# Differential attention and channel mixing on one core: moving the prologue's products, the maxima's steps and the last group's stages

## The chip, the cores and the metric

The kernel runs on 1 core of one Trainium2 chip. The metric is device microseconds of one execution; the median of the runs is compared. All times below are microseconds unless marked ns.

## The reference, cut to what matters

```python
# x: (2, 1024, 128); 16 heads, each with two score maps of width d = 4 and values of width 8
q, k, v = x @ Wq * d ** -0.5, x @ Wk, x @ Wv            # split into 32 score heads, 16 value heads
probs = softmax(where(causal, q @ k.T, -inf))            # 32 maps per batch, 1024 x 1024
attn = (probs[:, :, 0] - lam * probs[:, :, 1]) @ v       # lam from lq1, lk1, lq2, lk2
attn = attn * rsqrt(mean(attn ** 2) + eps) * rms_w * (1 - LAMBDA_INIT)
x = layernorm(x + attn @ Wo)
x_prev = shift x by one token                             # zeros ahead of token 0
r = sigmoid((mu_r * x + (1 - mu_r) * x_prev) @ W_r.T)
k = relu((mu_k * x + (1 - mu_k) * x_prev) @ W_k.T) ** 2
out = layernorm(x + r * (k @ W_v.T))
```

## The kernel before, in words

Each engine's program is written out by hand, in order; engines meet at counting semaphores only. The 64 score maps are worked off in 32 **pairs** (n = 0 to 31; two pairs are one group g, numbers pr 0 and 1; groups 0, 1, 14 and 15 are written out, the others stand in a loop of two groups, so four pairs for one turn of it).

**Splitting.** The scores must be exact, so q and k are cut in three bf16 parts (`high` and `middle` on ACT, `remainder` and `low` on DVE) and written to DRAM (`q_rows`, `k_rows`) as rows that SP loads again per pair (`load_max_rows` into `qm`, `km`, L288; `load_exp_rows` into `qe`, `ke`, L294). SP writes the q parts of the first 32 partitions, ACT the k parts (`write_parts`, L308), and SP then the rest of batch 0 and batch 1.

**Maxima.** For each pair there are NU = 9 units (`MAX_UNITS`): PE computes coarse scores into one of two PSUM buffers `mx` (`max_unit`, L557; unit m waits until unit m - 2 is reduced) and DVE reduces them (`max_unit`, L1047, one TENSOR_REDUCE over 1024 columns for each unit). Units 0 and 1 also add a mask. Then DVE runs `combine` (the maxima of all nine), `split_high` and `split_low` (row maximum in two bf16 parts); PE turns them (`turn_maxima`, L603), ACT copies them to `max_rows` (L877) and SP places them in `qe` by two small transfers (`place_maxima`, L300).

**Bursts.** A pair has NQ = 9 bursts b. PE does in each: a unit of maxima (unit 8 of pair n + 1 at b = 0, units 0 to 7 of pair n + 2 at b = 1 to 8, EARLY = 8), two score tiles in `ex` (L609; three PSUM banks in a ring, `ex_slot`), and a sum burst (L628) for the exponentials of four bursts ago (LAG = 4). ACT takes the exponential of each tile (L960), POOL masks the diagonal ones. Between these come, at fixed bursts: `take_sums` at b = 3 (ACT copies the sums of pair n - 1), `turn_maxima` for pair n + 1 at MAXIMA_AT = 4 behind the scores and its ACT copy behind both exponentials of that burst, `turn_sums` and `store_sums` at TURN_AT = 6, `invert` at INVERT_AT = 1 of the second pair of a group (DVE). A slot of the ring is kept for the turned maxima and two for the turned sums.

**SP's queue.** For each pair SP issues in this order, and waits in order: `load_max_rows(n + 2)`, `load_exp_rows(n + 1)` (once pair n - 1 is scored), `place_maxima(n + 1)` (once ACT has copied them). So the loads for pair n + 2 stand behind the placing for pair n.

**DVE's order** at the maxima of a pair: unit 8, `combine`, unit 0 of the next but one, `split_high`, unit 1, `split_low`, then units 2 to 7:

```python
                if m == NU - 1:
                    combine(n + 1, 1 - pr)
                if m == NU:
                    split_high(n + 1)
                if m == NU + 1:
                    split_low(n + 1)
```

**Prologue.** x is turned on PE; q and k are projected and split, chunk by chunk (ACT and DVE copy one chunk of xT of each batch); the 16 products for the values (L682) and three turned weights (L689) come next, and only then the maxima of pair 0 and 1 (17 units). `wait` on v_copied stands ahead of the first `turn_maxima`.

**Last group and tail.** In group 15 the stages of batch 0 are put beside the bursts by the tables `beside`: `turn_attn`, `project`, `turn_x1`, `ffn_k`, `ffn_r`, `ffn_o` on PE, `norm_attn`, `apply1`, `square_k`, `norm_ffn`, `apply2` on DVE, the roots on POOL. The token shift is done by two accumulated products, with weights scaled by mu and by 1 - mu (`w_cur`, `w_prev`). Pair 31's sums come in two halves (`normalise_half`, `root_half`, `place_half`). Then batch 1 (chunks 2 and 3) follows as a chain: turn, project, norm, turn, k, r, o, norm, store. `turn_attn(2)` stands between the last sum bursts.

Of the kernel before, what the change touches and what calls it, by code (L numbers as in the profile page):

```python
# [12 lines left out]
P = 128  # L13
# [77 lines left out]
TAKE_AT, TURN_AT, MAXIMA_AT, INVERT_AT = 3, 6, 4, 1  # L91
# [3 lines left out]
EX_BANKS = 3  # L95

# [21 lines left out]
def build(nc, x, Wq, Wk, Wv, Wo, lq1, lk1, lq2, lk2, rms_w, W_r, W_k, W_v, mu_r, mu_k, out):  # L118
# [24 lines left out]
    with ExitStack() as ctx:  # L143
# [12 lines left out]
        w_cur = sb("w_cur", [P, 2, P])  # L156
        w_prev = sb("w_prev", [P, 2, P])
# [82 lines left out]
        def mx_of(n, pr, m):  # L240
# [11 lines left out]
                   x1_turned x1_copied k_scored r_scored k_relued r_gated k_squared o_scored z_scaled z_ready  # L252
                   stats2 rooted1 rooted2 half_set half_steps half_rooted shifted1 shifted2 quad_seen
                   den_inverted values_seen norm_seen norm_steps lam_paired out_ready
# [53 lines left out]
        def write_parts(eng, which, b, own, done):  # L308

            subs = slice((b * P + own.start) // D, (b * P + own.stop) // D)  # L310
            for part, need in ((0, "hi_done"), (1, "mid_done"), (2, "lo_done")):
                eng.wait_ge(s[need], 4 * (b + 1))
                for w in which:
                    for i in (i for i, term in enumerate(TERMS) if term[w] == part):
                        eng.dma_start((q_parts, k_parts)[w][subs, :, i, :], parts[w][part][own, b, :])\  # L315
                            .then_inc(done, 16)

        @block.sync
        def _(sp):
# [23 lines left out]
            write_parts(sp, (0,), 0, slice(0, HEAD), s["rows_head"])  # L343
# [4 lines left out]
            write_parts(sp, (0, 1), 0, slice(HEAD, P), s["rows_b0"])  # L348
            fill_rows(1, s["rows_b1"])
            write_parts(sp, (0, 1), 1, slice(0, P), s["rows_b1"])  # L350
# [34 lines left out]
        def _(pool):  # L385
# [156 lines left out]
            beside = {(0, 2): [(root1, 0)], (0, 8): [(root1, 1)], (1, 7): [(root2, 0)], (1, 8): [(root_half, 0)]}  # L542
# [8 lines left out]
            for stage, arg in ((root2, 1), (root_half, 1), (root1, 2), (root1, 3), (root2, 2), (root2, 3)):  # L551
                stage(arg)
# [3 lines left out]
        def _(pe):  # L556
# [46 lines left out]
            def turn_maxima(n, bank):  # L603

                pe.wait_ge(s["max_split"], n + 1)
# [56 lines left out]

            pe.wait_ge(s["ident"], 5)
            for b in range(B):
                pe.wait_ge(s[f"x_in{b}"], 16)
                for t in range(b * NB, (b + 1) * NB):
                    last = pe.transpose(wide[t // 4][:, P * (t % 4):P * (t % 4 + 1)], x_tok[:, t, :], identf[:])
                    if t % 4 == 3:
                        last.then_inc(s["xt_done"], 1)
                if b == 0:  # L670
                    pe.wait_ge(s["wqk_in"], 32)
                for ch in (2 * b, 2 * b + 1):
                    pe.wait_ge(s["xt_copied_a" if ch % 2 == 0 else "xt_copied_d"], b + 1)
                    for w, weights in enumerate((wq_sb, wk_sb)):
                        m = 2 * ch + w
                        wait(pe, s["rest_done"], m - 3)
                        pe.matmul(narrow[m % 4], weights[:], xT[:, BANK * ch:BANK * (ch + 1)], start=True,  # L677
                                  stop=True).then_inc(s["proj_done"], 1)
            pe.wait_ge(s["wv_in"], 16)
            pe.wait_ge(s["rest_done"], 2 * NCH)  # L680
            for t in range(NT):
                last = pe.matmul(narrow[t // 4][:, P * (t % 4):P * (t % 4 + 1)], xT[:, P * t:P * (t + 1)],  # L682
                                 wv_sb[:], start=True, stop=True)
                if t % 4 == 3:
                    last.then_inc(s["v_done"], 1)
# [11 lines left out]
            for m in range(NU):  # L697
                max_unit(0, 0, m)
# [573 lines left out]
```

## Time and profile before

| | |
|---|---|
| median of 3 runs | 464.49 (463.41 to 464.81) |
| profiled execution, its own time | 463.41 |
| its span in the profile | 461.6, so 1.8 lie around it |
| mean granted TensorE clock | 0.941 |
| first exponential, last reduction of a unit | 53.7, 388.6 |
| busy: PE, DVE, ACT, POOL | 397.3, 393.2, 352.2, 223.4 |

A row of the timeline gives start, duration, engine, line and tiles, and in brackets the idle time of the engine before it and who ended it. Merged rows (x7) hold several instructions in turn. A landing time counts from the issue of a transfer to its last byte. The ends of matmuls are modelled.

### The profile page before, as it was taken

The numbers are of one execution on the slowest core, as the hardware profiler recorded it, in microseconds if no ns is written. First come the engines' busy times: TensorE is split into PE (matmuls) and PEld (weight loads), VectorE is DVE, ScalarE is ACT, GpSimd is POOL, SyncE is SP. The second block draws the span as 40 slices with busy tenths as digits, with TensorE's granted clock in tenths as the row PEclk, the third lists the DMA queues.
The fourth block names the chain that finished last, engine by engine and source line by source line (L and its number), as shares of the span: only waits on it lengthen the run. The fifth ranks groups of instructions, "written<-read, shape, count | busy, mean of one in ns | idle before, by whom it ended". The sixth has DMA issues, their size and how long they took to land.

```text
span 461.6 us, 16566 instructions
## 1 busy us (share of the span) xinstructions
PE 397.3 (86%) x5717; PEld 192.1 (42%) x5717; DVE 393.2 (85%) x554; ACT 352.2 (76%) x735; POOL 223.4 (48%) x514
## 2 busy tenths in 40 slices
PE   5475699999989999999999999999999999995682
PEld 2152234444444444444444444444444444553452
DVE  1459999999999999999999999999999998435443
ACT  2360389899989989999989999998999999763233
POOL 7200122356555656555555556565656565663312
PEclk9795589999999999999999999999999999999578
DMA  5468311111111111111111211111111110000101
GB/s 134 171 217 323 134 49 48 49 48 50 48 49 48 46 46 46 46 47 47 46 48 55 51 49 50 46 56 49 55 47 46 48 48 26 3 1 2 45 1 45
DMA packets 21390, 28.44 MB, mean 62 GB/s; under 512 B 4960, under 2 KB 9952, under 8 KB 21232
## 3 DMA queue, kind: packets, MB, share of 16 engines
q1 hardware_dynamic: 20688, 27.45, 19.8%
q10 hardware_dynamic: 672, 0.59, 0.4%
q8 instruction: 19, 0.31, 0.3%
q14 instruction: 11, 0.09, 0.1%
HBM read 20.39 MB, written 9.47 MB: 65 GB/s over the span
## 4 chain that ended last, share of the span: by engine, by line
PE 70%; ACT 11%; DVE 9%; issue 5%; ACTq 2%; DMA 1%; POOL 0%; POOLq 0%; DVEq 0%
PE acc L652 32%; PE mx L570 14%; ACT e_buf L960 9%; PE ex L622 9%; DVE part_max L1054 5%; PE ex L660 3%; PE mx L579 2%; PE ex L677 2%; PE ex L606 2%; PE mx L742 1%; DMA x_tok<-in_L_attn_x 1%; PE mx L743 1%; PE mx L727 1%; ACTq L315 1%; PE mx L762 1%
## 5 line engine op out<-in xcount | busy, mean ns | idle before, releaser
L1054 DVE TENSOR_REDUCE part_max<-mx 128x2 f32<-128x1024 f32 (+2 forms) x288 | 336.7, 1214 | 5.9 <-PE mx L570 3.8
L960 ACT ACTIVATE e_buf<-ex 128x512 f32<-128x512 f32 x576 | 304.8, 599 | 43.7 <-PE ex L622 41.0
L491 POOL TENSOR_SCALAR_AFFINE_SELECT e_buf<-e_buf 128x256 f32<-128x256 f32 x256 | 99.5, 407 | 175.2 <-ACT e_buf L960 175.2
L652 PE MATMUL acc<-e_buf,v_grp 128*32 128x256 f32 x2756 | 181.0, 351 | 0.1
L622 PE MATMUL ex<-qe,ke 26*128 26x512 bf16 (+3 forms) x768 | 139.3, 332 | 0.6 <-ACT e_buf L960 0.6
L570 PE MATMUL mx<-km,qm 29*128 29x128 bf16 (+3 forms) x1280 | 117.4, 270 | 15.6 <-DVE part_max L1054 13.0
L570 PEld LDWEIGHTS mx<-km,qm 26*128 26x128 bf16 (+1 forms) x1280 | 41.8, 93 | 118.3 <-DVE part_max L1054 79.3
L652 PEld LDWEIGHTS acc<-e_buf,v_grp 128*32 128x32 f32 x2756 | 64.6, 108 | 52.6 <-issue 36.3
L622 PEld LDWEIGHTS ex<-qe,ke 26*128 26x128 bf16 x768 | 45.0, 91 | 12.2 <-ACT e_buf L960 3.0
L474 POOL TENSOR_TENSOR r_rms<-sq_eps,minus_half 128x16 f32<-128x16 f32 x15 | 43.6, 2906 | 0.1
L579 PE MATMUL mx<-mask,pick 32*128 32x128 bf16 x512 | 25.9, 220 | 0.0
L881 ACT COPY max_rows<-ex 32x128 bf16<-32x128 bf16 x32 | 7.9, 248 | 13.8 <-PE ex L606 13.8
L579 PEld LDWEIGHTS mx<-mask,pick 32*128 32x128 bf16 x512 | 17.9, 96 | 0.0
L606 PE MATMUL ex<-identb,turn_max 128*128 128x128 bf16 x32 | 7.4, 231 | 12.1 <-ACT e_buf L960 11.3
L520 POOL TENSOR_TENSOR rs<-ve,minus_half 128x4 f32<-128x4 f32 x8 | 8.2, 1024 | 18.8 <-DVE ve L1145 18.8
L660 PE MATMUL ex<-identf,o_rows 128*128 128x128 f32 x62 | 13.6, 300 | 3.0
L888 ACT COPY o_rows<-acc 128x256 f32<-128x256 f32 x31 | 11.5, 372 | 4.5 <-PE acc L652 2.5
L479 POOL TENSOR_TENSOR attn_n<-attn,r_rms 128x32 f32 (+1 forms) x60 | 12.9, 247 | 3.7 <-POOL r_rms L474 3.7
L436 POOL COPY v_grp<-v_all 128x128 f32 (+1 forms) x16 | 4.6, 290 | 18.6 <-ACT v_all L864 18.6
L677 PE MATMUL ex<-xT,wq_sb 128*128 128x512 f32 x8 | 6.4, 894 | 6.8 <-ACT xT L836 6.8
L606 PEld LDWEIGHTS ex<-identb,turn_max 128*128 128x128 bf16 x32 | 3.1, 96 | 21.7 <-issue 17.0
L660 PEld LDWEIGHTS ex<-identf,o_rows 128*128 128x128 f32 x62 | 6.2, 140 | 12.1 <-ACT e_buf L960 11.9
(134 smaller groups left out, 269.9 us busy)
## 6 DMA issues: line engine op xcount, KB each, us to landing
qm<-q_rows SPq DMA_DIRECT2D x32, 128.0 KB, 2.6
km<-k_rows SPq DMA_DIRECT2D x32, 128.0 KB, 2.7
qe<-q_rows SPq DMA_DIRECT2D x32, 128.0 KB, 2.5
ke<-k_rows SPq DMA_DIRECT2D x32, 128.0 KB, 2.7
q_rows<-part_q SPq DMA_DIRECT2D x6, 256.0 KB, 5.5
k_rows<-part_k SPq DMA_DIRECT2D x6, 256.0 KB, 5.4
q_rows<-part_q SPq DMA_DIRECT2D x6, 192.0 KB
k_rows<-part_k SPq DMA_DIRECT2D x6, 192.0 KB
```

The lines of the kernel that those rows point to most:

```text
L474: pool.tensor_tensor(r_rms[:], sq_eps[:], minus_half[:], ALU.pow).then_inc(s["norm_steps"], 1)
L479: pool.tensor_tensor(attn_out(n, c, ab), attn_chunks[:, c, ab], r_rms_chunks[:, c, ab], ALU.mult).then_inc(s["attn_ready"], 1)
L491: pool.affine_select(out=e, in_=e, compare_op=ALU.is_ge, fill=0.0, base=0, pattern=[[0, PAIR], [1, P]], channel_multiplier=-1)\
L570: last = pe.matmul(bank[:, jj, col:col + P * nk], qm[pr][rows, P * qb:P * (qb + 1)], km[pr][rows, P * kb:P * (kb + nk)], start=i == 0, sto ...
L579: last = pe.matmul(bank[:, jj, :].rearrange("p (a t) -> p a t", a=4)[:, :, own], pick[rows, c, :], cols, start=False, stop=c == 3, skip_gr ...
L606: pe.transpose(ex[:, bank, :].bitcast(BF16)[:, 0:P], turn_max[:].rearrange("p e r -> p (e r)"), identb[:]).then_inc(s["max_turned"], 1)
L622: scored = pe.matmul(ex[:, ex_slot(b, i) % EX_BANKS, col:col + w], ke[pr][rows, P * kb:P * (kb + 1)], qe[pr][rows, q1 - w:q1], start=col = ...
L652: last = pe.matmul(out, v, e, start=first, stop=over, skip_group_check=True)
L660: last = pe.transpose(turned[:, P * i:P * (i + 1)], o_rows[pr][:, P * i:P * (i + 1)], identf[:])
L677: pe.matmul(narrow[m % 4], weights[:], xT[:, BANK * ch:BANK * (ch + 1)], start=True, stop=True).then_inc(s["proj_done"], 1)
L960: nc.scalar.activation(e_buf[:, b, i, :], ex[:, ex_slot(b, i) % EX_BANKS, :], ACT.Exp).then_inc(s["exped"], 1)
L1054: nc.vector.tensor_reduce(target, mx_of(n, pr, m)[:].rearrange("p s (a b) -> p s a b", a=a), AX.X, ALU.max).then_inc(s["maxed"], 1)
```

## The change

- Prologue: SP and ACT share the first writes in another way (8 and 4 instead of 6 and 6); DVE, not ACT, copies chunk 2 of xT; the maxima's units begin directly behind the projections. The value products stand one by one behind units 3 to 16 on PE, in the order of chunks 2, 3, 0, 1; the weights are turned behind unit 13, now in `acc`; `turn_maxima(0)` comes behind unit 12. ACT copies also unscaled weights (`w_both`). On DVE the last five splitting steps and lambda's steps stand between and behind the units.
- Steady part: `combine`, `split_high` and `split_low` one unit later; MAXIMA_AT 4 to 5, TURN_AT 6 to 7, INVERT_AT 1 to 2.
- Last group: for batch 0 DVE mixes the tokens (`mix_x`), so k and r need one product each; stages are placed anew.
- Tail: the last sums ahead of `turn_attn(2)`; `turn_x1(3)` ahead of `ffn_o(2)`; both halves normalised before chunk 2's norm; the last `apply2` shared by ACT and DVE (two tiles each).

```diff
-TAKE_AT, TURN_AT, MAXIMA_AT, INVERT_AT = 3, 6, 4, 1
+TAKE_AT, TURN_AT, MAXIMA_AT, INVERT_AT = 3, 7, 5, 2
+V_ORDER = (2, 3, 0, 1)
...
-            write_parts(sp, (0,), 0, slice(0, HEAD), s["rows_head"])
+            for w, part in ((0, 0), (1, 0), (0, 1)):
+                write_part(sp, w, part, 0, slice(0, HEAD), s["rows_head"])
...
+                if c == NCH - 1:
+                    sp.wait_ge(s["rest_ready"], 1)
...
-            beside = {(0, 2): [(root1, 0)], (0, 8): [(root1, 1)], (1, 7): [(root2, 0)], (1, 8): [(root_half, 0)]}
+            beside = {(0, 2): [(root1, 0)], (0, 7): [(root1, 1)], (1, 7): [(root2, 0)], (1, 8): [(root_half, 0)]}
...
-            for stage, arg in ((root2, 1), (root_half, 1), (root1, 2), (root1, 3), (root2, 2), (root2, 3)):
+            for stage, arg in ((root_half, 1), (root2, 1), (root1, 2), (root1, 3), (root2, 2), (root2, 3)):
...
+            def turn_weights():
+                pe.wait_ge(s["w_in"], 16 * 4)
+                pe.wait_ge(s["v_copied"], 2)
+                for i in range(3):
+                    last = pe.transpose(acc[:, P * i:P * (i + 1)], wf_sb[:, i, :], identf[:])
+                last.then_inc(s["wt_done"], 1)
...
+            values = {3 + i: [(V_ORDER[i // 4], i % 4)] for i in range(12)}
+            values[NU + EARLY - 2] = [(V_ORDER[3], 0), (V_ORDER[3], 1)]
+            values[NU + EARLY - 1] = [(V_ORDER[3], 2), (V_ORDER[3], 3)]
+            for u in range(NU + EARLY):
+                max_unit(0, u // NU, u % NU)
+                for ch, i in values.get(u, []):
+                    project_v(ch, i)
+                if u == NU + 3:
+                    turn_maxima(0, 2)
+                if u == NU + 4:
+                    turn_weights()
+            pe.wait_ge(s["wt_scaled"], 1)
             pe.wait_ge(s["v_copied"], NCH)
...
+                if ch < 2:
+                    pe.wait_ge(s["x_mixed"], 2 * ch + 1)
+                    pe.matmul(main[ch], w_both[:, 1, :], x_mixed[ch][:, 1, :], start=True, stop=True)\
+                        .then_inc(s["k_scored"], 1)
+                    return
...
+                    if ch < 2:
+                        last = pe.matmul(o, x_mixed[ch][:, 0, P * i:P * (i + 1)], w_both[:, 0, :], start=True, stop=True)
+                        continue
...
-                      (0, 4): [(project, 1)], (0, 8): [(turn_x1, 0)], (1, 0): [(ffn_k, 0)], (1, 1): [(turn_x1, 1)],
+                      (0, 4): [(project, 1)], (0, 8): [(turn_x1, 0)], (1, 0): [(turn_x1, 1)], (1, 1): [(ffn_k, 0)],
...
-            turn_attn(2)
             sum_burst(NG - 1, 1, 1, NQ - 2)
             sum_burst(NG - 1, 1, 1, NQ - 1)
             turn_sums(NPAIR + 1, 0, last_acc)
+            turn_attn(2)
             project(2)
             turn_attn(3)
             project(3)
...
+            turn_x1(2)
+            ffn_k(2)
+            ffn_r(2)
+            turn_x1(3)
+            ffn_o(2)
+            ffn_k(3)
+            ffn_r(3)
+            ffn_o(3)
...
+                last = nc.scalar.copy(w_both[:, i, :], src)
...
-            copy_attn(2)
             take_half(1)
             store_half(1)
+            copy_attn(2)
             copy_attn(3)
             apply1(2)
             copy_x1(2)
+            apply1(3)
             relu_k(2)
-            apply1(3)
             gate_r(2)
...
-            apply2(3)
+            apply2(3, 2)
...
+            late = {0: [(remainder, 6), (low, 5)], 1: [(remainder, 7), (low, 6)], 2: [(low, 7)],
+                    NU: [(combine, 0, 0)], NU + 1: [(split_high, 0)], NU + 2: [(split_low, 0)]}
+            for u in range(NU + EARLY):
+                max_unit(0, u // NU, u % NU)
+                for step, *args in late.get(u, []):
+                    step(*args)
+                if u == 4:
+                    lambda_dots()
+            lambda_pairs()
...
-                if m == NU - 1:
+                if m == NU:
                     combine(n + 1, 1 - pr)
-                if m == NU:
+                if m == NU + 1:
                     split_high(n + 1)
-                if m == NU + 1:
+                if m == NU + 2:
                     split_low(n + 1)
...
+            def mix_x(ch):
+                b, t0 = ch * BANK // S, ch * BANK % S
+                dve.wait_ge(s["xcol_set"], 1)
+                dve.wait_ge(s["x1_copied"], ch + 1)
+                wait(dve, s["x_mixed"], 2 * ch)
+                now, past = x1T[:, b, 1 + t0:1 + t0 + BANK], x1T[:, b, t0:t0 + BANK]
+                nc.vector.tensor_tensor(x_step[:], now, past, ALU.subtract).then_inc(s["x_stepped"], 1)
+                dve.wait_ge(s["x_stepped"], ch + 1)
+                for i in (1, 0):
+                    nc.vector.scalar_tensor_tensor(out=x_mixed[ch][:, i, :], in0=x_step[:], scalar=mu[:, i:i + 1],
+                                                   in1=past, op0=ALU.mult, op1=ALU.add).then_inc(s["x_mixed"], 1)
...
             apply1(1)
+            mix_x(0)
             invert(NG - 2, 0)
+            mix_x(1)
             square_k(0)
             norm_ffn(0)
             square_k(1)
+            norm_ffn(1)
             normalise_half(0)
-            norm_ffn(1)
+            apply2(0)
+            normalise_half(1)
             place_half(0)
-            apply2(0)
-
-            normalise_half(1)
+            place_half(1)
             norm_attn(2)
-            place_half(1)
             apply2(1)
```

## Rows read from the trace of the kernel before

**Rows 1.** Part 1 of the page: busy time of each engine, share of the span.
```profile
PE 397.3 (86%) x5717; PEld 192.1 (42%) x5717; DVE 393.2 (85%) x554; ACT 352.2 (76%) x735; POOL 223.4 (48%) x514
```

**Rows 2.** Timeline, DVE, one pair: start, us, engine, line, operation, tiles, [idle before].
```profile
226.47 8.06 DVE L1054 TENSOR_REDUCE part_max<-mx 128x2 f32<-128x1024 f32 x7
...
234.57 0.22 DVE L1060 TENSOR_REDUCE row_max<-part_max 128x16 f32<-128x64 f32 x1
...
234.80 1.23 DVE L1054 TENSOR_REDUCE part_max<-mx 128x8 f32<-128x1024 f32 x1
```

**Rows 3.** Timeline, PE: unit 0 at burst 1 of pair 1 and of pair 29.
```profile
66.34 0.40 PE L570 MATMUL mx<-km,qm 29*128 29x128 bf16 x8
...
377.91 0.34 PE L570 MATMUL mx<-km,qm 29*128 29x128 bf16 x6
```

**Rows 4.** Timeline, SP queue, two pairs; last, landing times of km's loads there.
```profile
217.22 1.19 SPq L305 DMA_DIRECT2D qe<-max_rows  x2
...
219.32 0.54 SPq L292 DMA_DIRECT2D km<-k_rows  x1
...
228.26 1.19 SPq L305 DMA_DIRECT2D qe<-max_rows  x2
...
230.67 0.54 SPq L292 DMA_DIRECT2D km<-k_rows  x1
...
DMA to landing us min/median/max: 2.6/2.6/2.6
```

**Rows 5.** Timeline, ACT, around burst 4 of the same pair.
```profile
226.49 1.58 ACT L960 ACTIVATE e_buf<-ex 128x512 f32<-128x512 f32 x3
...
227.94 0.25 ACT L881 COPY max_rows<-ex 32x128 bf16<-32x128 bf16 x1
```

**Rows 6.** Timeline, pair whose km lands late, with that load's landing time.
```profile
129.84 0.54 SPq L292 DMA_DIRECT2D km<-k_rows  x1
...
133.98 0.40 PE L570 MATMUL mx<-km,qm 29*128 29x128 bf16 x8 [0.73 <-DVE part_max L1054]
...
134.74 1.23 DVE L1054 TENSOR_REDUCE part_max<-mx 128x8 f32<-128x1024 f32 x1 [0.52 <-PE mx L579]
...
139.60 1.19 SPq L305 DMA_DIRECT2D qe<-max_rows  x2
...
DMA to landing us min/median/max: 4.0/4.0/4.0
```

**Rows 7.** Timeline, start of the kernel, with the landing time of rms_col.
```profile
21.69 0.60 SPq L292 DMA_DIRECT2D km<-k_rows  x1
...
34.17 10.28 DVE L1054 TENSOR_REDUCE part_max<-mx 128x8 f32<-128x1024 f32 x9 [0.99 <-PE mx L579]
...
45.34 0.61 SPq L352 DMA_DIRECT2D rms_col<-w_bounce  x1
...
54.06 0.61 PE L570 MATMUL mx<-km,qm 29*128 29x128 bf16 x8 [0.38 <-DVE part_max L1054]
...
DMA to landing us min/median/max: 5.0/5.0/5.0
```

**Rows 8.** Chain that ended last, in the last group: start, us, what.
```profile
403.49 0.86 PE mx L743 x2
...
414.80 0.22 PE mx L754 x2
...
439.03 0.87 PE mx L734 x4
```

**Rows 9.** Timeline, last group and tail.
```profile
414.25 0.69 DVE L1183 TENSOR_TENSOR xT<-part_k,x 128x512 f32<-128x512 f32 x1
...
421.78 0.25 DVE L1199 RECIPROCAL r_den<-o_tok 128x16 f32<-128x16 f32 x1 [4.72 <-ACT o_tok L910]
...
426.78 0.76 PE L719 MATMUL mx<-identf,attn_n 128*128 128x128 f32 x4 [4.39 <-DVE attn_n L1223]
...
457.36 1.65 ACT L936 ACTIVATE v_all<-xT,shift,rs 128x128 f32<-128x128 f32 x4 [3.17 <-POOL shift L527]
```

More of the change, by code:

```diff
@@ L156, in build @@
         w_cur = sb("w_cur", [P, 2, P])
+        w_both = sb("w_both", [P, 2, P])
+        x_step = sb("x_step", [P, BANK])
+        x_mixed = [sb(f"x_mixed{i}", [P, 2, BANK]) for i in range(2)]
         w_prev = sb("w_prev", [P, 2, P])
@@ L603, in turn_maxima @@
             def turn_maxima(n, bank):
+                if isinstance(n, int) and n == 0:
+                    pe.wait_ge(s["v_copied"], 1)
                 pe.wait_ge(s["max_split"], n + 1)
@@ L661, in turn_sums @@
                 last.then_inc(s["acc_turned"], 1)
-            pe.wait_ge(s["ident"], 5)
[L664 to L685, printed above, removed]
-            pe.wait_ge(s["w_in"], 16 * 4)
-            pe.wait_ge(s["v_copied"], 1)
-            for i in range(3):
-                last = pe.transpose(narrow[0][:, P * i:P * (i + 1)], wf_sb[:, i, :], identf[:])
@@ L690, in _, with turn_x, project_qk @@
-            last.then_inc(s["wt_done"], 1)
+            def turn_x(ch):
+                for t in range(4 * ch, 4 * ch + 4):
+                    last = pe.transpose(wide[ch][:, P * (t % 4):P * (t % 4 + 1)], x_tok[:, t, :], identf[:])
+                last.then_inc(s["xt_done"], 1)
+            def project_qk(m):
+                ch = m // 2
+                wait(pe, s["rest_done"], m - 3)
+                pe.matmul(narrow[m % 4], (wq_sb, wk_sb)[m % 2][:], xT[:, BANK * ch:BANK * (ch + 1)], start=True,
+                          stop=True).then_inc(s["proj_done"], 1)
@@ L820, in _ @@
             project(3)
-            for ch in (2, 3):
-                turn_x1(ch)
-                ffn_k(ch)
-                ffn_r(ch)
-                ffn_o(ch)
+            turn_x1(2)
[6 more added lines that the diff above has]
+            ffn_o(3)
         @block.scalar
@@ L1047, in max_unit @@
+            for i in range(2):
+                nc.vector.memset(part_max[i][:], NEG).then_inc(s["parts_set"], 1)
+            nc.vector.memset(turn_max[:, 2:], 0.0).then_inc(s["parts_set"], 1)
+            copy_x(1)
+            remainder(0)
+            for m in range(1, 4):
+                remainder(m)
+                low(m - 1)
+            low(3)
+            copy_x(2)
+            copy_x(3)
             def max_unit(g, pr, m):
@@ L1130, in _ @@
             group(NG - 2, 0)
-            for b in range(3):
+            for b in range(NU - EARLY + 3):
                 burst(NG - 1, 1, 0, b)
```

186 lines of the change are left out of this document (98 added, 88 removed).

## The prediction, made before the changed kernel was run

> **What bounds the kernel now.** I read the page first, then DVE's timeline over the steady part, then the queue of SP beside PE and ACT, and last the chain of waits for the tail. On the page no engine stands out: PE is busy for 86% of the span, DVE for 85% [rows 1]. The timeline shows where each is the bound. From unit 2 of one pair to the next pair's maxima DVE has no gap: seven reductions take 8.06, so one starts every 1.14, and `combine` begins at 234.57, when the last has ended, the next unit 0.23 later [rows 2]. That is a steady part in which DVE is full. From unit 0 at burst 1 of pair 1 to that of pair 29 PE needs 377.91 - 66.34 = 311.57 for 28 pairs, 11.13 each [rows 3]. These are 312 of 461.6. Before them lies the prologue (66), behind them the last pairs and the tail (84).
>
> One more loop runs through every pair, and the reader is to see it because no engine's busy share shows it: ACT copies the turned maxima, SP places them, and only then does SP issue qm and km for the pair after next; PE needs these at its burst 1. Placing starts at 217.22 and the km load is issued 2.10 later, at 219.32; where the program's loop turns (once in four pairs) it is 2.41 [rows 4]. The load lands 2.6 after its issue [rows 4].
>
> How close this loop is, one pair tells: there km took 4.0 to land. It was issued at 129.84, PE could start unit 0 at 133.98 only, 0.14 after the landing, and DVE then stood idle for 0.52 [rows 6]. So a normal km comes 4.0 - 2.6 = 1.4 earlier and has some 0.9 to spare before DVE stands still.
>
> **The steady part, where the change costs.** Three things move by a burst. `combine` goes behind unit 0 of the next pair: it need no longer wait for unit 8 to end. Now 8.06 / 7 = 1.15 per unit, plus 0.04, plus 0.23 stand for it; behind another unit I put 0.15 for it, so DVE would save 0.1 to 0.2 in each pair, if DVE stayed the bound. The Trainium skill, VectorE: DVE Perf Modes, section The DRAIN you can't avoid, says that the next operation waits for the pipe to empty with or without a semaphore; by that rule nothing would be saved here. The rows speak for a little, and it will not matter if the loop below binds. `invert` keeps its price.
>
> The turn of the maxima goes from burst 4 to burst 5. Its ACT copy then stands behind two more exponentials. Three of them in a row take 1.58 and one lasts 0.60, so one starts every 0.49, and the copy at 227.94 starts behind the third, bound by ACT, not by the turn [rows 5]. Two more are 0.98. They are no added work, but they stand ahead of the copy, and behind the copy stand, on SP, the two placing transfers and then qm and km of the pair after next.
>
> So the loop is, counted from PE's start of unit 0 at burst 1:
> - to the placing now: 139.60 - 133.98 = 5.62 [rows 6]; this is PE's own bursts 1 to 3 and `take_sums`, then ACT, so it does not depend on DVE;
> - two exponentials more: 0.98 [rows 5];
> - placing to the issue of km: 2.10, with the loop's turn 0.31 more in one pair of four, 0.08 on average [rows 4];
> - landing 2.6 [rows 4] and PE's start 0.14 after it [rows 6].
>
> Sum 11.52 per pair. Today the same sum is 10.54, below the 11.13 of the pair, so the loop has slack of 0.6; after the change it is above and becomes the bound: 11.52 - 11.13 = 0.39 more per pair. The loads for pairs 3 to 31 are gated so; from burst 1 of pair 1 to that of pair 29 are 28 pairs: **+10.9**. Bounds for the pair: 11.35 (landing 2.5, the copy a little nearer) and 11.7 (a late landing as in rows 6 now and then), so +6 to +16. `turn_sums` at burst 7 and its place in the ring of `ex` have the same structure as now, a burst later, and cost nothing: the copies on ACT lie one in each of the bursts 3, 5 and 7; cover gone, they would be 0.3 each. POOL gets the inverted sums a burst later and masks nothing at bursts 3 to 6, which is enough.
>
> **The prologue, where it gains.** Rows of pair 0 are loaded from 21.69 and 2.7 more on they are there, near 24.4, but the first reduction is at 34.17 and the nine take 10.28 [rows 7]. After the change units can start near 25. DVE does five splitting steps of 0.69 between the first three units (3.4) and lambda's steps (0.8), so its 17 units end at about 25 + 17 x 1.14 + 4.4 = 49, not 53.9. That is 4.8 earlier, but two things come later than that. SP's queue is a row of issues without a gap up to rms_col, 45.34 + 0.61 = 45.95 [rows 7]; the sharing of the first writes (8 issues on SP, 4 on ACT) makes the last of them 0.2 earlier, and so all behind it. Placing for pair 0 can start at 45.7; km for pair 2 is issued 2.1 later and lands at 50.5 or, as much of batch 1 is still being written (rms_col took 5.0 to land [rows 7]), near 51. DVE also waits for rms_col, to about 50.1. The copies of the values (the last two products stand behind units 15 and 16), the weights and the two extra copies to `w_both` end near 48 and are hidden by that. So PE's burst 1 of pair 0 moves from 54.06 [rows 7] to about 50.8. Bounds: 48.5 if the rows land at once, 52 if they wait for all writes. At burst 1 of pair 1 this leaves **-3.3** (-5 to -2).
>
> **Last group and tail, where it gains more.** In each chunk of batch 0 the second k product (0.86) and four of eight r products (0.22 each) fall away [rows 8]: 2 x (0.86 + 0.88) = 3.5 on PE, which is the chain there. DVE gets three operations of 128x512 for each chunk; a like one takes 0.69 [rows 9], 2.1 in all, and it is idle for several us between its steps there; they come between the copy of x1 and ffn_k, and one burst more has been put there. `turn_x1(1)`, one burst sooner, comes up to 0.5 before its x1. That leaves -3.0 at the first half's sums. Then the last sums run at once: now `turn_attn(2)` waits for 4.39 [rows 9] with the last two sum bursts behind it. But the second half's store, some 8 earlier, is not what ends last: DVE has `norm_ffn(1)`, both halves and `apply2(0)` in a row. From normalising half 0 to `turn_attn(2)` are 426.78 - 421.78 = 5.0 today [rows 9], with `norm_ffn(1)` in between. After the change half 1 (I put 1.8 for its seven small steps) and `apply2(0)` (1.1, as ACT's four tiles take 1.65 [rows 9]) come before it too: 7.9 from the start of that norm near 417.2 (3.0 before where it could start now), so `turn_attn(2)` at 425.1, only 1.7 earlier. What follows is shorter: projecting 2 no longer waits behind half 1, and `turn_x1(2)`, now at 439.03 behind `project(3)` [rows 8], starts about 434.4: -4.6. `turn_x1(3)` ahead of `ffn_o(2)` hides its copy (0.6 with the hand-over): -5.2. The last four tiles on ACT take 1.65 [rows 9]; with two on DVE -0.8. Sum **-5.9** (-7.5 to -4). PE stands idle for over 3 ahead of `turn_attn(2)` after the change as before it, so I take the tail's products at the same granted clock. Pair 30 itself is free of the loop: -0.1.
>
> **Sum.** -3.3 + 10.9 - 0.1 - 5.9 = +1.6. The profiled execution took 463.41 (span 461.6 and 1.8 around it), so it would be 465.0; the median shown, 464.49, lies 1.1 above it, so **466.1** there. A change of about 0.3% (1.4) is what a measurement of this kernel can tell from none.
>
> **Rivals.**
> - A, DVE stays the bound (0.12). If the placing is sooner than I say, a pair takes 10.95 by DVE's saving: 28 x -0.18 = -5.0, with -9.3 at the ends -14.3: 450.2. For it: DVE has no gap now [rows 2]. Against it: rows 6, where 1.4 of lateness already stops it. The Trainium skill, Perfetto Trace Analysis, section Identifying the Most-Contended Engine, would have one take work off the busiest engine first; by it this case would come out. [...]
> - B, the loop just fits (0.18). Its slack today is 0.6 by my sum and 0.9 by rows 6; were it 0.98, pairs would stay at 11.13, and only the ends count: 464.5 - 9.3 = 455.2.
> - C, slower (0.12): the placed maxima come late too. Half of `place_maxima` is issued 0.6 behind its start; it must land by burst 0, some 1.15 before burst 1, which by the loop is 4.84 behind the placing. If it takes over 3.7 from the start of the placing, each 0.1 beyond it costs 2.8 in all. With a pair at 11.8: +18.8 - 9.3 = +9.5: 474.0.
> - The change does not do what it says (0.03): the units start no earlier, as SP's rows are late: 3 more than forecast, 469.
>
> **Chances.** Forecast 0.55, with a range of its own of 462.5 to 469.5: within it 0.30 slower, 0.18 same, 0.07 faster. With A and B faster, C and the last case slower: faster 0.37, same 0.18, slower 0.45. The range for all is 454.5 to 470: it takes in B and most of the forecast's cases and leaves A and most of C out.
>
> **What would show it.** Unit 0 at burst 1: 28 periods of about 11.5, DVE idle about 0.4 to 0.6 in each pair just before it, with PE named, and PE idle there with km's landing 0.1 earlier; SP's placing 6.6 after PE's burst 1. First exponential near 50. Last group: k with one product, turn_attn(2) behind all sums, one shared last apply. Periods of 11.13 or less, with no idle time at burst 1, make the forecast wrong by 10 or more; a span unchanged with such short periods would put the fault in my ends.

## The result, and where the time went

The changed kernel takes **472.44** us (470.75 to 474.43), the kernel before 464.09 beside it on the same chip: a ratio of 1.018, 95% interval 1.014 to 1.022. I had forecast slower by 1.6, that is 466.1, with a range up to 470.0: the side was right, the time lies 2.4 above the range. The profiled execution has a span of 470.6 (before: 461.6). Burst 1 of pairs 1 and 29 cuts both into three parts:

| part | before | after | difference | forecast |
|---|---|---|---|---|
| start to burst 1 of pair 1 | 66.34 | 65.20 | -1.1 | -3.3 |
| 28 pairs | 311.57 (11.13 each) | 327.17 (11.68 each) | +15.6 | +10.9 |
| burst 1 of pair 29 to the end | 83.69 | 78.23 | -5.5 | -6.0 |

The page of the changed kernel, parts 1 and 5 (busy time; costliest groups with their idle time before):

```profile
PE 411.2 (87%) x5697; PEld 193.0 (41%) x5697; DVE 400.3 (85%) x563; ACT 351.6 (75%) x734; POOL 224.7 (48%) x514
...
L1112 DVE TENSOR_REDUCE part_max<-mx 128x2 f32<-128x1024 f32 (+2 forms) x288 | 340.5, 1214 | 27.1 <-PE mx L590 20.0
...
L581 PE MATMUL mx<-km,qm 29*128 29x128 bf16 (+3 forms) x1280 | 118.2, 272 | 19.9 <-DMA km<-k_rows 10.6
```

Beside [rows 1] hardly a busy share has moved. What is new is the last field: DVE, which had no gap in the pair of [rows 2], stands idle for 27 us before its reductions (5.9 in the kernel before), mostly because PE is late, and PE is late because of km. Part 4, the chain that ended last, says the same; at 14% the landing of km is its largest piece (in the kernel before, DMA had 1% of the chain and PE 70%):

```profile
PE 36%; issue 15%; DMA 15%; DVE 12%; SPq 10%; ACT 10%; POOL 1%; ACTq 1%; DVEq 1%; POOLq 0%
```

One turn of the loop, from the timelines of PE, SP's queue and DVE (start, us, engine, line, what, idle time before):

```profile
218.37 0.40 PE L581 MATMUL mx<-km,qm 29*128 29x128 bf16 x8 [0.30 <-DMA km<-k_rows]
...
225.05 1.19 SPq L310 DMA_DIRECT2D qe<-max_rows  x2
...
227.15 0.54 SPq L297 DMA_DIRECT2D km<-k_rows  x1
...
229.88 0.40 PE L581 MATMUL mx<-km,qm 29*128 29x128 bf16 x8 [0.29 <-DMA km<-k_rows]
...
230.63 1.23 DVE L1112 TENSOR_REDUCE part_max<-mx 128x8 f32<-128x1024 f32 x1 [0.47 <-PE mx L590]
```

In the same pair on ACT:

```profile
222.32 2.56 ACT L1011 ACTIVATE e_buf<-ex 128x512 f32<-128x512 f32 x5
224.72 0.26 ACT L884 COPY max_rows<-ex 32x128 bf16<-32x128 bf16 x1
```

From PE's burst 1 to the placing 6.68 (it was 5.62, [rows 6]), to the issue of km 2.10, to the next burst 1 2.73: 11.51. DVE then has its 0.47 of idle time, with PE named. The combine does overlap now: the next unit starts 0.13 behind it, where [rows 2] have 0.23 (DVE, same pair):

```profile
220.26 0.21 DVE L1118 TENSOR_REDUCE row_max<-part_max 128x16 f32<-128x64 f32 x1
220.39 1.22 DVE L1112 TENSOR_REDUCE part_max<-mx 128x8 f32<-128x1024 f32 x1
```

So both the wait and the overlap that the forecast named are there; the sizes are taken up below.

The head, PE between the last maxima units of the prologue and at the first bursts of pair 0, then ACT's last copy of values:

```profile
47.56 0.61 PE L581 MATMUL mx<-km,qm 26*128 26x256 bf16 x4
48.10 1.22 PE L692 MATMUL ex<-wv_sb,xT 128*128 128x128 f32 x4
49.26 0.61 PE L581 MATMUL mx<-km,qm 26*128 26x256 bf16 x4
49.79 1.22 PE L692 MATMUL ex<-wv_sb,xT 128*128 128x128 f32 x4
51.74 0.50 PE L581 MATMUL mx<-km,qm 26*128 26x128 bf16 x6 [0.72 <-issue]
...
52.01 0.76 PE L581 MATMUL mx<-km,qm 26*128 26x128 bf16 x10
52.55 0.33 PE L590 MATMUL mx<-mask,pick 32*128 32x128 bf16 x2
...
53.67 0.60 PE L581 MATMUL mx<-km,qm 29*128 29x128 bf16 x8
```

A merged row carries the shape of its first instruction. The sixteen products in the rows at 51.74 and 52.01 are the eight of unit 8 (burst 0) and the eight of unit 0 (burst 1), whose mask follows at 52.55; the first of unit 0 starts at 52.12. The row at 53.67 is unit 1, at burst 2. So burst 1 of pair 0 comes at 52.12, where the kernel before has 54.06 [rows 7] and the forecast 50.8.

```profile
51.05 0.58 ACT L904 COPY v_all<-ex 128x512 f32<-128x512 f32 x1 [2.54 <-PE ex L692]
```

The same products in the kernel before, ahead of the maxima, and in the changed one (groups by line, busy us and mean ns of one; each product is two records):

```profile
L682 PE MATMUL ex<-wv_sb,xT 128*128 128x128 f32 x24 | 2.9, 278 | 2.0 <-DVE rest L1014 2.0
L682 PE MATMUL acc<-wv_sb,xT 128*128 128x128 f32 x8 | 1.1, 275 | 0.0
```

```profile
L692 PE MATMUL ex<-wv_sb,xT 128*128 128x128 f32 x24 | 8.8, 487 | 0.1
L692 PE MATMUL acc<-wv_sb,xT 128*128 128x128 f32 x8 | 3.2, 502 | 0.0
```

And the changed kernel's window from 44 to 48 (busy time of PE, PEld, DVE, ACT, POOL; then the granted clock):

```profile
44.00:48.00 4.00, 4.00 (x18) 1.96 (x17) 3.17 (x3) 1.85 (x9) 0.00 (x0) 0.50 1.05 403
```

PE is full there, at the lower of its two levels (1.2 GHz), and DVE waits for it: its 17 units end at 51.1 and not at 49. The last two products end at 51.0, the copy stands behind them until 51.6, and PE waits for the copy before the first burst of pair 0. What that wait costs is taken up below.

### The profile page after: what moved, and what is told of

The parts are those of the page before. It is cut to its first block, busy times and chain, and to the rows that moved or that the text cites. A ratio compares the mean times of both kernels' runs of the same rounds, so it can differ in the third digit from the quotient of the medians.

```text
span 470.6 us, 16533 instructions
## 1 busy us (share of the span) xinstructions
PE 411.2 (87%) x5697; PEld 193.0 (41%) x5697; DVE 400.3 (85%) x563; ACT 351.6 (75%) x734; POOL 224.7 (48%) x514
## 4 chain that ended last, share of the span: by engine, by line
PE 36%; issue 15%; DMA 15%; DVE 12%; SPq 10%; ACT 10%; POOL 1%; ACTq 1%; DVEq 1%; POOLq 0%
DMA km<-k_rows 14%; PE acc L665 10%; PE mx L581 9%; ACT e_buf L1011 7%; DVE part_max L1112 7%; SPq L310 5%; PE ex L635 4%; SPq L296 3%; PE mx L590 2%; PE ex L692 1%; SPq L318 1%; DMA x_tok<-in_L_attn_x 1%; DVE turn_max L1125 1%; ACT max_rows L884 1%; PE mx L805 1%
## 5 line engine op out<-in xcount | busy, mean ns | idle before, releaser
L1112 DVE TENSOR_REDUCE part_max<-mx 128x2 f32<-128x1024 f32 (+2 forms) x288 | 340.5, 1214 | 27.1 <-PE mx L590 20.0
L502 POOL TENSOR_SCALAR_AFFINE_SELECT e_buf<-e_buf 128x256 f32<-128x256 f32 x256 | 100.8, 412 | 166.7 <-ACT e_buf L1011 166.7
L635 PE MATMUL ex<-qe,ke 26*128 26x512 bf16 (+3 forms) x768 | 147.7, 335 | 0.7 <-ACT e_buf L1011 0.5
L635 PEld LDWEIGHTS ex<-qe,ke 26*128 26x128 bf16 x768 | 46.2, 91 | 22.4 <-ACT e_buf L1011 9.0
L490 POOL TENSOR_TENSOR attn_n<-attn,r_rms 128x32 f32 (+1 forms) x60 | 12.8, 245 | 3.7 <-POOL r_rms L485 3.7
L1249 DVE SCALAR_TENSOR_TENSOR part_k<-part_k,mx 128x512 f32<-128x512 f32 x4 | 2.8, 688 | 8.6 <-PE mx L805 8.6
L463 POOL TENSOR_TENSOR o_scaled<-o_tok,r_lam 128x256 f32<-128x256 f32 x15 | 9.5, 632 | 1.2
```

The source lines that it names most:

```text
L490: pool.tensor_tensor(attn_out(n, c, ab), attn_chunks[:, c, ab], r_rms_chunks[:, c, ab], ALU.mult).then_inc(s["attn_ready"], 1)
L502: pool.affine_select(out=e, in_=e, compare_op=ALU.is_ge, fill=0.0, base=0, pattern=[[0, PAIR], [1, P]], channel_multiplier=-1)\
L635: scored = pe.matmul(ex[:, ex_slot(b, i) % EX_BANKS, col:col + w], ke[pr][rows, P * kb:P * (kb + 1)], qe[pr][rows, q1 - w:q1], start=col = ...
L1112: nc.vector.tensor_reduce(target, mx_of(n, pr, m)[:].rearrange("p s (a b) -> p s a b", a=a), AX.X, ALU.max).then_inc(s["maxed"], 1)
```

## Experiments

The executions of a table row ran beside executions of the kernel before (medians 463.7 to 464.0); "burst 1" is that of pair 1, the period is over 28 pairs, "rest" is from burst 1 of pair 29 to the end, all from the profiled execution alone. How far such a single reading scatters, the table itself shows: with the same prologue and the same order on SP burst 1 comes at 65.20 (the changed kernel), 65.67, 63.03 and 64.81, and with the same tail the rest takes 77.6 to 79.4.

| kernel | median | ratio, 95% | burst 1 | period | rest |
|---|---|---|---|---|---|
| steady_old | 457.80 | 0.981 to 0.988 | 65.67 | 11.18 | 77.9 |
| steady_new | 480.42 | 1.027 to 1.037 | 66.51 | 11.70 | 84.6 |
| loads_first | 455.91 | 0.979 to 0.985 | 63.59 | 11.13 | 78.9 |
| before_loads_first | 463.53 | 0.997 to 1.002 | 65.29 | 11.10 | 84.1 |
| turn_old | 468.78 | 1.007 to 1.015 | 63.03 | 11.64 | 78.8 |
| max4_late | 478.27 | 1.020 to 1.037 | 64.81 | 11.88 | 79.4 |
| lf_max4 | 476.73 | 1.022 to 1.032 | 64.36 | 11.89 | 78.7 |
| lf_combine_old | 458.01 | 0.977 to 0.993 | 64.34 | 11.17 | 79.0 |
| lf_values_short | 454.82 | 0.970 to 0.987 | 63.26 | 11.13 | 77.6 |
| lf_values_early | 455.54 | 0.980 to 0.988 | 63.29 | 11.13 | 78.5 |
| lf_two_products | 460.03 | 0.988 to 0.994 | 64.39 | 11.13 | 82.5 |
| lf_tail_order_old | 458.37 | 0.984 to 0.993 | 64.61 | 11.13 | 80.9 |
| best_a | 454.39 | 0.976 to 0.981 | 64.79 | 11.10 | 77.9 |
| best_b | 455.16 | 0.976 to 0.982 | 63.92 | 11.11 | 78.9 |

### Is it the steady part?

**steady_old** is the changed kernel with

```diff
-TAKE_AT, TURN_AT, MAXIMA_AT, INVERT_AT = 3, 7, 5, 2
+TAKE_AT, TURN_AT, MAXIMA_AT, INVERT_AT = 3, 6, 4, 1
-                if m == NU:        combine; NU + 1: split_high; NU + 2: split_low
+                if m == NU - 1:    combine; NU: split_high; NU + 1: split_low
```

> The changed kernel with the five schedule positions of its steady loop put back (turn, maxima, invert at 6, 4, 1 in place of 7, 5, 2; the combine, split high and split low behind the last scoring unit of a half group as before); prologue and tail stay changed. Theory (the steady loop costs the time): the period of a pair falls from 11.69 to 11.13 us, 28 pairs give back 15.6 us, span near 455 and time near 457, about 7 us faster than the kernel before (ratio 0.985). Rival (the later positions are innocent, the cost comes in with the prologue's or the clock's state and stays with the chip through the loop): the period stays at 11.6 to 11.7 and the time near 472.

**steady_new** is the kernel before with the same edit the other way round.

> The kernel before with only the five schedule positions of the steady loop changed. Theory: the period of a pair goes from 11.13 to 11.69 us, +15.6 us over 28 pairs, time near 480 (ratio 1.033). Rival (the loss needs the new prologue or tail beside it): under 470.

Measured: 457.80 and 480.42, periods 11.18 and 11.70. The steady part costs some 15 whichever prologue and tail stand beside it. (11.18 and not 11.13 holds two pairs of 12.5 and 12.4 right behind the prologue: PE waited 1.24 for a late km at 78.16, and then had a granted clock of 0.58 from 79 to 83. In the other 26 pairs the period is 11.09.)

### Is it the loop through SP?

**loads_first** changes only the order of SP's issues in the changed kernel, for pair 0 too:

```diff
+            load_max_rows(sp, 2, 0)
             place_maxima(sp, 0, 0, 0)
...
-                    load_max_rows(sp, n + 2, pr)
                     load_exp_rows(sp, n + 1, 1 - pr)
+                    load_max_rows(sp, n + 3, 1 - pr)
                     place_maxima(sp, n + 1, 1 - pr, g + pr)
```

> The changed kernel with one edit on the SP queue: the loads of the query and key rows of pair n+3 are issued ahead of the placing of the maxima of pair n+1, right behind the loads of its exponential rows, in place of behind it. The loop that my forecast names (first burst of a pair, placing of the maxima, issue of the next key rows, landing, first burst of the next pair) is then cut, since the key rows no longer wait for the placing. Loop theory: the period falls from 11.69 to 11.1 us or less (the bound is VectorE again), so 15 us or more off, time near 456. Rival (the later positions cost through VectorE's or the ring's order or through TensorE, and the late key rows are only a symptom): the period stays above 11.5 and the time above 467.

**before_loads_first** is the same edit of the kernel before.

> The same edit of the SP queue in the kernel before. Theory (in the kernel before VectorE bounds the loop and the key rows land in time): within 1 us of the kernel before, 463 to 465. Rival (its key rows were also late in some pairs, so that the order of the queue costs there too): 2 to 5 us faster, period under 11.05.

Measured: 455.91 (-16.5 on the changed kernel) and 463.53 (no change). The placing is as late as before, 6.60 to 6.72 behind burst 1, but km is issued ahead of it and PE starts without it. DVE is without a gap again:

```profile
224.43 8.16 DVE L1116 TENSOR_REDUCE part_max<-mx 128x2 f32<-128x1024 f32 x7
232.51 0.21 DVE L1122 TENSOR_REDUCE row_max<-part_max 128x16 f32<-128x64 f32 x1
232.63 1.22 DVE L1116 TENSOR_REDUCE part_max<-mx 128x8 f32<-128x1024 f32 x1
233.77 0.38 DVE L1129 CAST turn_max<-row_max 128x16 bf16<-128x16 f32 x1
```

So the loss of the steady part is the loop, all but some 0.03 a pair: with it cut in both, the period is 11.13 here and 11.10 in the kernel before. That the same edit gives nothing before shows that its loop had slack.

### Which of the moves closes the loop?

**turn_old** is the changed kernel with 3, 6, 5, 1: only the maxima's turn and the combine stay late.

> The changed kernel with the sums' turn and the inversion back at 6 and 1, and only the turn of the maxima (5) and the combine's place as in the change. Loop theory: the placing of the maxima still stands two exponentials later, so the period of a pair stays at 11.6 to 11.7 us. Rival (the delay of the sums' turn, with its place in the ring of score banks, has a part in it): period under 11.5.

Period 11.64, so the turn of the maxima closes the loop. The 11.64 holds two long pairs, 12.54 and 12.75, around a late km; over pairs 7 to 28, which have none in either kernel, it is 11.55 against 11.62 in the changed kernel. So the sums' turn and the inversion have a small part, some 0.06 a pair. It shows in every second pair: there SP places 6.73 behind burst 1 in the changed kernel and 6.55 in turn_old. In those pairs of the changed kernel PE waits at burst 4 for POOL, which gets the inverted sums a burst later, in 11 pairs from 5 to 27:

```profile
234.00 0.64 PE L665 MATMUL acc<-e_buf,v_grp 128*32 128x256 f32 x8 [0.24 <-POOL v_grp L447]
```

In turn_old that wait is 0.04 at most.

**max4_late** is the changed kernel with 3, 7, 4, 2: the maxima's turn early, the combine late.

> The changed kernel with only the turn of the maxima back at burst 4; combine and splits stay a unit later. Loop theory: the placing comes 5.6 to 6.1 us behind PE's burst 1 in place of 6.7, the sum of the loop is 10.6 to 11.1, so the period falls to 11.1 to 11.2 (some 14 us off, time near 458). Rival (TensorE now waits at burst 4 for the low split, which VectorE does a unit later, and the pair pays that on TensorE): period 11.3 or more.

Measured 478.27, period 11.88: the rival, and worse than it said. The placing is back at 5.64 to 5.76, so the loop is short again, yet PE now waits for the low split (PE's timeline):

```profile
235.03 0.23 PE L619 MATMUL ex<-identb,turn_max 128*128 128x128 bf16 x1 [1.24 <-DVE turn_max L1130]
```

and behind that wait the clock goes (windows; PE, PEld, DVE, ACT, POOL, clock):

```profile
233.00:235.00 2.00, 0.80 (x16) 0.29 (x6) 2.00 (x6) 1.89 (x5) 1.85 (x5) 1.00 0.00 0
235.00:237.00 2.00, 1.97 (x23) 0.79 (x25) 1.48 (x2) 0.88 (x3) 1.62 (x5) 0.63 0.01 2
237.00:239.00 2.00, 2.00 (x30) 0.85 (x22) 1.67 (x2) 1.52 (x4) 0.22 (x1) 0.51 0.10 26
239.00:241.00 2.00, 2.00 (x27) 0.78 (x24) 1.89 (x3) 1.57 (x4) 0.22 (x1) 1.00 0.35 108
```

From pair 5 on, pairs of 11.26 alternate with pairs of 12.8. In ten of the odd ones the granted clock falls to the lower level, 1.2 GHz, for some 3 us behind a wait of 1.10 to 1.24. In two of them, pairs 9 and 23, it stayed at 1.00 behind waits of 1.23 and 1.24, and these took 11.58: so the clock costs 1.2 in a pair in which it falls. After the waits of up to 0.92 in the other pairs it never fell. **lf_max4** asks whether the loop has a part in that, by taking it away (loads first, and 3, 7, 4, 2):

> The kernel with the loads first and the turn of the maxima back at burst 4, combine and splits a unit later. Theory (TensorE's wait for the low split, and the granted clock behind it, cost the pair): TensorE still waits about 1 us at burst 4 and the pair takes 11.5 to 11.9. Rival (with burst 4 the loop was still the cause): 11.1 to 11.2.

Period 11.89, and in eleven odd pairs the clock falls as before (0.72 from 211 to 217); in the one left, pair 15, it stays up behind a wait of 1.21, and that pair takes 11.58. The loop has no part in it. A late combine needs a late turn of the maxima, or PE stops and is slowed.

### What is the combine's move worth?

**lf_combine_old** is loads_first with combine and splits at their old places:

> The kernel with the loads first on the SP queue (pair 11.12 us, VectorE without idle time), with only the combine and the two splits back at their old places. My forecast put 0.1 to 0.2 us per pair of VectorE's time on the move, if VectorE stays the bound: then the pair takes 11.22 to 11.32 here. Rival (the move only shifts the same cost: 0.11 less at the combine, 0.17 more at the following cast): 11.05 to 11.12.

Period 11.17, between the two: 0.04 per pair, about 1 us in all, in place of 0.1 to 0.2. The overlap of the combine saves 0.1 (0.13 for 0.22 from its start to the next unit's). Part of that is lost again at the splits: the low split takes 0.21 in place of 0.16. The cast of `split_high`, which the expectation's rival names, is not where it goes: it takes 0.35 with the combine back at its old place and 0.37 in loads_first. It takes 0.21 in the kernel before and in best_a below, which has all the old positions, so its length comes with the later turns; why is open. The placing 0.08 later in every second pair of this run (6.79 for 6.72) was not followed up.

### Why the head gave 1.1 and not 3.3

**lf_values_short** is loads_first with quarter-length value products:

```diff
-                xT[:, P * t:P * (t + 1)], wv_sb[:],
+                xT[...].bitcast(BF16)[upper halves], wv_sb[:].bitcast(BF16)[upper halves],
```

> The kernel with the loads first, in which each value product is made from the upper halves of its operands as bf16, a product of a quarter of the passes: this makes the values inexact, and takes some 4.5 of the 6.3 us that the sixteen products take between the first maxima at the half clock. If the products there are why burst 1 of pair 0 came at 52 to 53.7 us and not at 50.8 as I forecast, it comes at 50 to 51 now. Rival (rows and queue of SP, or the maxima placed, set it): 52 or later.

The "52 to 53.7 us" of this expectation, and the 52.3 of the next one, are a misreading of mine: they are the starts of unit 1 at burst 2. Burst 1 of pair 0 comes at 50.79 in loads_first and at 52.12 in the changed kernel. The row of twelve in loads_first holds the last four products of unit 8 and the eight of unit 0:

```profile
50.58 0.86 PE L585 MATMUL mx<-km,qm 26*128 26x128 bf16 x12
```

With the short products it comes at 50.61, next to nothing sooner:

```profile
50.02 0.61 PE L639 MATMUL ex<-qe,ke 26*128 26x512 bf16 x2 [2.29 <-DMA qe<-max_rows]
50.61 0.61 PE L585 MATMUL mx<-km,qm 29*128 29x128 bf16 x8
```

PE and DVE are done sooner (DVE's last unit of the prologue starts at 46.46 and not at 48.58), but PE then waits 2.29 for the placed maxima. So the rival named the cause, if not its number: the placed maxima hold the scores of burst 0 at 50.02, where products and copy had them at 50.55. (The full products take 12.0 of PE in the changed kernel and not the 6.3 of my expectation.)

**lf_values_early** is loads_first with the values in the order 0, 1, 2, 3, the first eight products ahead of the first unit and the others behind units 3 to 10.

> The kernel with the loads first, with the value products of chunks 0 and 1 ahead of the first maxima, while TensorE waits for the first rows at 20 to 23.5 us, and those of chunks 2 and 3 behind units 3 to 10, none behind the last two units. The last value copy then no longer stands between the maxima and the first scores of pair 0. If TensorE's products and that copy set burst 1 of pair 0, it comes 1 to 2 us earlier than in the kernel with the loads first (52.3) and the time is 454 to 455. Rival (the placed maxima's landing sets it at once): within 0.5 us, time 455.9.

The same picture with exact values: burst 1 of pair 0 at 50.79, as in loads_first, of pair 1 at 63.29, time 455.54, within 0.5 of loads_first: the rival. PE again waits for the placed maxima:

```profile
50.66 0.61 PE L639 MATMUL ex<-qe,ke 26*128 26x512 bf16 x2 [1.87 <-DMA qe<-max_rows]
```

Behind that the clock is at its lower level:

```profile
48.00:52.00 4.00, 1.83 (x31) 1.36 (x34) 3.10 (x9) 0.72 (x2) 0.00 (x0) 0.50 0.63 192
52.00:56.00 4.00, 3.85 (x35) 1.53 (x39) 4.00 (x7) 3.89 (x9) 1.94 (x5) 0.50 0.15 49
56.00:60.00 4.00, 4.00 (x51) 1.52 (x43) 2.92 (x3) 2.62 (x7) 0.00 (x0) 0.60 0.00 1
60.00:64.00 4.00, 3.81 (x70) 1.57 (x70) 3.93 (x5) 3.35 (x7) 1.04 (x3) 1.00 0.16 45
```

PE is full from 52 to 60, at half its clock until about 59. In the changed kernel the lower level lasts until 62.1, 10.0 behind burst 1 of pair 0, and pair 0 takes 13.08; in the kernel before it lasts until 62.0, 7.9 behind it, and pair 0 takes 12.28. That fits the 0.8 of the head's gain that is gone between pairs 0 and 1: what starts earlier runs longer at the slow clock. It is read from the windows; no run holds the clock apart.

### The two terms of the tail

**lf_two_products** takes the branches for batch 0 out of `ffn_k` and `ffn_r`:

```diff
-                if ch < 2:
-                    pe.matmul(main[ch], w_both[:, 1, :], x_mixed[ch][:, 1, :], start=True, stop=True)
```

> The kernel with the loads first, with the k and r products of batch 0 made twice as before (with the current and with the previous token) and the mixing on VectorE kept but not waited for. My forecast put 3.0 us of the tail's gain on the single products: from burst 1 of pair 29 to the end 78.2 becomes 81. Rival (TensorE is not the chain there): under 79.

**lf_tail_order_old** puts the four engines' last steps back in their old order:

> The kernel with the loads first, with the order of the last steps put back on TensorE, ScalarE, VectorE and GpSimd (attention chunk 2 turned ahead of the last two sum bursts, the halves normalised around the norm of chunk 1, each chunk of the last two finished before the next begins); single products and the shared last apply stay. My forecast put 2.2 us on this order: 78.2 becomes 80.4. Rival (the order only moves idle time): under 79.

Measured 82.5 and 80.9 against 78.9: the single products are worth 3.6, the order 2.0, each within the scatter of such readings, 77.6 to 79.4 for one and the same tail. Forecast: 3.0 and 2.2. The shared last apply takes 0.88 on ACT where it took 1.65 [rows 9], the 0.8 of the forecast. What still stands in the tail of the changed kernel is the wait that the forecast kept (PE's timeline):

```profile
439.57 1.11 PE L752 MATMUL mx<-identf,attn_n 128*128 128x128 f32 x4 [3.43 <-DVE attn_n L1293]
```

### Versions that beat both

**best_a**: new prologue and tail, old steady positions, loads first.

> New prologue and tail, the old positions of the steady loop (6, 4, 1 and the early combine), and the loads first on the SP queue. If the parts add: the kernel with loads first (455.9) less the 0.04 us per pair by which its pair (11.13) is above that of the kernel before with loads first (11.08 to 11.09): 454.5 to 455.5. Rival (something of the late positions was needed by the rest): above 456.5.

**best_b**: the same with the early values, the placing of pair 0 first on SP, and DVE's wait for rms_col behind the first group.

> The former with the value products of chunks 0 and 1 ahead of the first maxima and the rest behind units 3 to 10, the placing of pair 0 ahead of the loads for pair 2 on SP, and VectorE's wait for the rms column behind the first group. If the head can be had: burst 1 of pair 0 near 49.5, of pair 1 near 61.5, 1.5 to 2 us less than the former, about 453. Rival (what starts earlier runs longer at the half clock, as in the two runs with short or early values): burst 1 of pair 1 at 63 and the time within 0.7 us of the former.

454.39 and 455.16 in six executions each, 2.2% and 2.1% below the kernel before; between the two no difference can be told. best_a took what its parts said (454.5 to 455.5), to 0.1. In best_b burst 1 of pair 0 came at 51.96 and of pair 1 at 63.92. The placing was ahead of the loads, as in the changed kernel, and burst 1 then waited for km of pair 2, which landed at 51.91:

```profile
51.96 0.61 PE L585 MATMUL mx<-km,qm 29*128 29x128 bf16 x8 [0.44 <-DMA km<-k_rows]
```

So in either order on SP's queue one of its landings stands next to the copy of the values.

## Point by point

- **The bound now** (DVE in the steady part, a loop through ACT, SP and DMA beside it that no busy share shows): the loop beside it is right: cutting it in the kernel before changed nothing, cutting it in the changed one gave back 16.5. That DVE is the bound without it rests on its having next to no gap (busy for 246.1 of the 250 us from 100 to 350 in the kernel before). PE is busy for 234.5 of the same 250, the chain that ended last runs through PE for 70%, and 0.1 less on DVE gave only 0.04, so how far DVE alone sets the 11.1 is not shown.
- **The loop's closing**: right in kind, too small by 0.17 a pair. "Sum 11.52 per pair" was the step that failed, and with it the range; over the 28 pairs the sum is 11.685. The placing comes 6.72 behind burst 1 and not 6.60, from km's issue to burst 1 it is 2.81 and not 2.74, and from the placing to the issue 2.15 for 2.18: (0.12 + 0.07 - 0.03) x 28 = +4.5 of the +4.7 that were missing. The bound of +16 held, the range of the whole did not, as the head missed in the same direction. "Two exponentials more: 0.98" held: ACT starts five in a row at 222.32 and copies the maxima at 224.72, 2.40 later, for 1.45 with three [rows 5]. What I had wrong are two things that the sum has at nothing.
  - "POOL gets the inverted sums a burst later ..., which is enough": it is not. PE waits 0.24 for POOL in 11 pairs, and in every second pair the placing comes 0.18 later than in turn_old: over 14 pairs 2.5, as an estimate, and 1.8 by the periods of the two kernels (0.06 x 28).
  - A late landing, which only the upper bound allowed for, is now paid in full, and then again in clock. One km took 3.7 to land; PE waited 1.38 for it, and that pair took 12.64. Behind the wait the granted clock fell, the next placing came 7.68 behind burst 1, and the next pair took 12.27. Against the 11.62 of the other 26 pairs that is 1.7. (In the kernel before, a landing of 4.0 made a pair of 11.92, with no fall of the clock.)

```profile
77.84 0.40 PE L581 MATMUL mx<-km,qm 29*128 29x128 bf16 x8 [1.38 <-DMA km<-k_rows]
```

```profile
79.00:83.00 4.00, 3.88 (x53) 1.61 (x50) 3.56 (x7) 2.86 (x7) 1.53 (x4) 0.57 0.00 0
```

- **The combine's saving**: it does overlap. The next unit starts 0.08 before the combine's end (220.39 for 220.47). The Trainium skill (VectorE: DVE Perf Modes, The DRAIN you can't avoid) has the next operation wait until the pipe is empty, but adds that one that is not held starts earlier; of this the forecast took the first half only. The trace shows the earlier start. The saving would have been 0.04 a pair, by the run without the move, and not 0.1 to 0.2.
- **The head**: -1.1 for -3.3, in two steps. Burst 1 of pair 0 came at 52.12 and not at 50.8, and pair 0 took 13.08 where I had counted on the 12.28 of the kernel before. For the first, "the copies of the values ... end near 48 and are hidden by that" failed as it stands: the last copy ended at 51.6. I priced the products at nothing behind DVE's 1.14 per unit, but the sixteen keep PE busy for 12.0 there at a clock of 0.50, for 4.0 in one stretch at 1.00 in the kernel before; the mean record is 1.8 times as long (487 ns for 278), and what putting them one by one between other products adds was not run by itself. Yet the copy cost little: km of pair 2 was issued at 48.74 and not at 47.8 and landed at 51.56, which allows burst 1 no sooner than 51.7 (estimate, with the 0.14 of [rows 6]), and taking the products away in loads_first moved burst 1 by 0.2. SP's queue was as much behind: the placing at 46.89 and not at 45.7. This scatters: in the three other runs with this prologue and this order on SP the placing starts at 44.57 to 46.76 and burst 1 of pair 0 comes at 50.59 to 51.81, so 50.8 is inside what the prologue can give. The second step is no scatter: pair 0 takes 12.44 to 13.86 in these four runs, and 12.09 to 12.28 in the three with the old prologue, most likely as more of it lies at the lower clock. The forecast took a gain at pair 0 for one at pair 1.
- **Tail**: -5.5 for -6.0 with pair 30 (the terms of the "Sum -5.9" add up to -6.0); the products 3.6 (forecast 3.0), the order 2.0 (2.2). `turn_attn(2)` waited 3.43, the "over 3" of the forecast. The mechanism was right, and the size too, as far as readings that scatter by 1.8 can tell.
- **Rivals**: A and B needed a placing earlier than it is; loads_first is what B's world looks like, and its 455.9 is near B's 455.2. A's saving of 0.18 a pair is not there even so (11.13). C's price (11.8 a pair) was nearer than the forecast's, but not its cause: PE waited for km, not for the placed maxima.

## To carry to other kernels

When a step is moved later on one engine, follow what is queued behind it on the queues, not only on the engines: here two small placing transfers stood ahead of a 128 KB load, and a loop of 10.5 in a period of 11.1 left 0.6 of slack for a delay of 1.1. Cutting such a loop (issue the load that depends on nothing ahead of the one that waits) was worth 16.5 here, where trimming it by 0.18 in every second pair (turn_old) gave some 2. A saving on the bounding engine of 0.1 per period is no reason to lengthen a loop that is some 5% below the period.

Work put "under" another engine has to be priced at the clock of that stretch: products that kept PE busy for 4.0 in one run at the upper level kept it busy for 12.0 between the maxima. But before blaming it for a late start, look what else ends at the same time: here a copy, the placed maxima and a load of keys stood close together, and taking one away gave 0.2.

A merged row of a timeline can hold the start that you look for. Count its instructions against the program before you take the next row.

## What I had not expected

- A single wait of a PE that is otherwise full can be followed by some 3 us at the lower clock. In pairs 5 to 27 of max4_late and lf_max4 that was so behind 21 waits of 1.10 to 1.24 and not behind three of 1.21 to 1.24, nor behind any of 0.92 or less; in the changed kernel, steady_old and turn_old it was so behind waits for km of 1.38, 1.24 and 1.33. The fall costs 1.2 in its pair, more than the wait itself costs, and made the kernel with the shorter loop (11.88) slower than the one with the long loop (11.68).
- In the head, an earlier start brought the upper clock earlier by less or not at all: it came back at 59.2 to 60.9 for starts of pair 0 at 50.6 to 50.8, at 62.1 for 52.12 and at 62.0 for 54.06, in the kernels after and before.
- The same cast of 128x16 takes 0.21 on average in the kernel before and 0.37 in loads_first, with no idle time named before it, and 0.35 with the combine at its old place.
